# A graph network's last edge pass: edge terms loaded first, table rows gathered onto them by DMA

## The reference

```python
row, col = (edge_index[0], edge_index[1])
h = jnp.concatenate([x[row], edge_attr], axis=1)
h = jax.nn.relu(h @ W1a + b1a) @ W1b + b1b
sums = jax.ops.segment_sum(h, col, num_segments=n_nodes)
counts = jax.ops.segment_sum(jnp.ones((h.shape[0],), dtype=h.dtype), col, num_segments=n_nodes)
agg = sums / jnp.clip(counts, 1.0)[:, None]
z = jnp.concatenate([x, agg, u[batch]], axis=1)
return jax.nn.relu(z @ W2a + b2a) @ W2b + b2b
```

## Time and profile before

| | |
|---|---|
| median of 3 runs | 9359.47 us (9359.37 to 9371.02) |
| profiled execution, first to last instruction (its span) | 9364.4 us |
| first block of the edge pass, within that span | 7146.9 to 8963.4 us |
| PE busy | 7028.5 us (75%) |
| DVE busy | 5660.6 us (60%) |
| POOL busy | 2656.2 us (28%) |
| ACT busy | 2515.7 us (27%) |

### The profile page before, as it was taken

The page is one execution under the profiler, slowest core; times in us unless marked ns, Lnnn a source line. Parts: engine busy times, 40 slices in busy tenths (PEclk is TensorE's granted clock), DMA queues, the critical chain, the costliest instruction groups (busy, mean ns, idle before and its releaser), DMA issues. The chain is left out here.

```text
span 9364.4 us, 133857 instructions
## 1 busy us (share of the span) xinstructions
PE 7028.5 (75%) x35740; PEld 4596.9 (49%) x35792; DVE 5660.6 (60%) x16783; ACT 2515.7 (27%) x5863; POOL 2656.2 (28%) x2952
## 2 busy tenths in 40 slices
PE   4777777775566659940488699999998777777787
PEld 4555555453122224420477544444445666666676
DVE  6777777775589990059899800000014777777786
ACT  0222222222467740020388600000001333310001
POOL 0777777776470000000000000000002444444410
PEclk9767776766679989975799899999999999999998
DMA  3333333334975538849566478787886766642363
GB/s 99 103 103 105 105 104 103 105 105 167 393 231 164 168 114 306 299 195 426 205 215 216 144 262 276 262 287 256 295 284 200 181 180 179 179 111 63 63 178 88
DMA packets 969628, 1759.77 MB, mean 188 GB/s; under 512 B 102288, under 2 KB 665125, under 8 KB 905315
## 3 DMA queue, kind: packets, MB, share of 16 engines
q1 hardware_dynamic: 683820, 1335.73, 44.1%
q0 software_dynamic: 110720, 276.01, 9.0%
q10 hardware_dynamic: 174394, 139.51, 5.5%
HBM read 1412.04 MB, written 338.80 MB: 187 GB/s over the span
## 5 line engine op out<-in xcount | busy, mean ns | idle before, releaser
L768 POOL DMA_INDIRECT bucketed<-arena,wide x1563 | 1515.6, 970 | 726.5 <-issue 714.0
L1920 PE MATMUL psum<-wide,arena 128*128 x6496 | 1209.9, 329 | 400.5 <-DVE arena L1979 393.9
L1920 PEld LDWEIGHTS psum<-wide,arena 128*128 128x128 f32 x6496 | 989.9, 195 | 618.3 <-issue 493.3
L1787 POOL DMA_DIRECT2D table<-wide x13 | 9.7, 743 | 4316.2 <-DVE wide L1711 4316.2
L1979 DVE TENSOR_SCALAR arena<-wide,tile_first 128x128 f32 x3248 | 870.8, 300 | 472.3 <-PE psum L1920 293.8
L1841 POOL DMA_INDIRECT arena<-table,src_i x832 | 803.3, 966 | 1009.1 <-PE psum L1937 872.4
L1660 PE MATMUL psum<-arena,h 128*128 128x512 f32 (+1 forms) x2548 | 1048.6, 570 | 19.1 <-DMA arena<-adjacency 17.5
L922 PE MATMUL psum<-arena 128*128 128x512 bf16 x2253 | 695.7, 442 | 435.0 <-DVE arena L870 259.4
L665 PE MATMUL psum<-arena 128*113 128x177 bf16 x1568 | 534.4, 341 | 416.2 <-ACT wide L687 374.6
L870 DVE TENSOR_SCALAR arena<-sums 128x512 bf16<-128x512 int16 x2304 | 799.9, 347 | 0.0
L659 PE MATMUL psum<-w_edge,arena 128*128 128x256 f32 x1568 | 786.9, 597 | 0.0
(11 more groups left out here) (398 smaller groups left out, 11006.0 us busy)
## 6 DMA issues: line engine op xcount, KB each, us to landing
arena<-adjacency SPq DMA_DIRECT2D x294, 1024.0 KB
arena<-adjacency SPq DMA_DIRECT2D x98, 1568.0 KB, 7.8
adjacency<-wide SPq DMA_DIRECT2D x588, 256.0 KB
arena<-adjacency SPq DMA_DIRECT2D x196, 640.0 KB, 3.9
arena<-adjacency SPq DMA_DIRECT2D x147, 768.0 KB
arena<-bucketed POOLq DMA_DIRECT2D x208, 528.0 KB, 6.0
arena<-adjacency SPq DMA_DIRECT2D x49, 1792.0 KB, 6.9
arena<-adjacency SPq DMA_DIRECT2D x49, 1344.0 KB, 6.1
```

The lines of the kernel that those rows point to most:

```text
L768: e.indirect_dma_start(bucketed, bass.IndirectOffsetOnAxis(ap=places[k][0:size, c:c + 1], axis=0), rows[k][0:size, c, :], None).then_inc(s ...
L1920: e.matmul(flat[:, ds((chunk & 3) * 512 + 2048, P)], lhsT=hot[:, i % 8, :], rhs=table_in[:, ds(tile * P, P)], start=False, stop=True, skip ...
```

## The change

The second ring `edge_in` is gone. SyncE loads the edge terms straight into `ring`, once TensorE is done with what the slot held. GpSimd waits for that landing and gathers with `compute_op=ALU.add`, so that the DMA adds the table rows to what is in the slot. VectorE's addition `message(n)`, its semaphore `s_sum` and the two waits ahead of it are gone; `rectify(n)` waits for the gathers itself, behind `looks(n)`.

```diff
             ring = slots(PAIR * P, DEEP).rearrange("p k (c w) -> p k c w", c=PAIR)
-            edge_in = slots(PAIR * P, DEEP).rearrange("p k (c w) -> p k c w", c=PAIR)
...
                 @block.gpsimd
                     for n in range(FAR_PAIRS):
                         k = n % DEEP
-                        if n >= DEEP:
-                            e.wait_ge(s_pe, n - DEEP + 1)
+                        e.wait_ge(s_side[k], 16 * (n // DEEP + 1))
                         for c in range(PAIR):
                             chunk = (NEAR_PAIRS + n) * PAIR + c
-                            e.indirect_dma_start(ring[:, k, c, :], None, table,
-                                                 bass.IndirectOffsetOnAxis(ap=src_i[:, chunk:chunk + 1], axis=0)).then_inc(s_got[k], 16)
+                            e.indirect_dma_start(ring[:, k, c, :], None, table, bass.IndirectOffsetOnAxis(ap=src_i[:, chunk:chunk + 1], axis=0),
+                                                 compute_op=ALU.add).then_inc(s_got[k], 16)
...
                 @block.sync
                         if n >= DEEP:
-                            e.wait_ge(s_sum, n - DEEP + 1)
-                        e.dma_start(edge_in[:, k, :, :], bucketed_v[:, cols(NEAR_PAIRS + n), 0:D]).then_inc(s_side[k], 16)
+                            e.wait_ge(s_pe, n - DEEP + 1)
+                        e.dma_start(ring[:, k, :, :], bucketed_v[:, cols(NEAR_PAIRS + n), 0:D]).then_inc(s_side[k], 16)
...
                 @block.vector
-                    def message(n):
+                    def rectify(n):
                         k = n % DEEP
                         e.wait_ge(s_got[k], 16 * PAIR * (n // DEEP + 1))
-                        e.wait_ge(s_side[k], 16 * (n // DEEP + 1))
-                        e.tensor_tensor(ring[:, k, :, :], ring[:, k, :, :], edge_in[:, k, :, :], ALU.add).then_inc(s_sum, 1)
-
-                    def rectify(n):
-                        k = n % DEEP
-                        e.wait_ge(s_sum, n + 1)
                         e.tensor_scalar(ring[:, k, :, :], ring[:, k, :, :], 0.0, None, op0=ALU.max).then_inc(s_msg, 1)
...
-                        message(n)
                         if n * PER_PAIR < LOOKS:
                             looks(n)
                         rectify(n)
```

More of the change, by code:

```diff
@@ L1813, in edge_pass @@
             s_side = [sem(f"meta_side{k}") for k in range(DEEP)]
-            s_hot, s_sum, s_msg, s_pe, s_add = (sem("meta_" + n) for n in ("hot", "sum", "msg", "pe", "add"))
+            s_hot, s_msg, s_pe, s_add = (sem("meta_" + n) for n in ("hot", "msg", "pe", "add"))
             sage_groups, sage_loads = 3 * GROUPS, 3 * len(PASSES) * TILES
```

## The result

| | before | after |
|---|---|---|
| median | 9365.92 us (9359.37 to 9377.30, 16 runs) | 9386.92 us (9369.29 to 9398.45, 16 runs) |
| profiled execution, its span | 9364.4 us | 9376.4 us |
| last scatter of the first stage starts (line 768) | 2256.2 us | 2269.0 us |
| first block of the edge pass | 7146.9 to 8963.4 us | 7158.2 to 8975.05 us |
| length of that block | 1816.5 us | 1816.9 us |

The ratio is 1.0019, with a 95% interval of 1.0012 to 1.0027: slower by 11 to 25 us. The block that the change edits (from SyncE's first load in it to its first load in the next one) is as long as it was.

A forecast was written before the change was run, and what follows sets the result against it. TensorE's queue was taken to bound the block. Start -4.0, steady state 0 and end +2.3 gave -1.7 us, from 9359.5 to 9357.8, and 9357 us with a small part of the busy stretch's waits; range 9338 to 9385.

The forecast's parts named there:

- The bound of the block: First block of the edge pass: TensorE's queue of look-ups and register loads is the chain, 4.25 us a quiet pair.
- The addition is worth 0 for each pair: VectorE in each pair: removing its 416 ns addition gains 0 us, as register loads before the first look hide it.
- Order of load and gather, 0: Each pair's gathers now wait for edge terms: 13.7 us at most, inside the ring's 34 us, so cost 0.
- 36 us for "VectorE, or longer register loads": Busy stretch, 240 pairs: 0.15 us a pair of extra TensorE waiting; none taken as gain; rival chance 0.09.
- Issue and transfer of the gathers, 0: GpSimd and DMA engines: adding gathers issue in under 1.5 us, DMA share at most 0.81, all hidden, cost 0.
- Steady state: 0: All pairs between the block's start and end: 0 us of change, between -36 and 0.
- The start, -4.0: Block's start: looks no longer wait behind message(0) for the first gathers, so they begin 4.0 us earlier.
- the 7.15 us: First gather's duration at the block's start, put down to standing behind VectorE's memset; otherwise the gain is about 2 us.
- The end, +2.3, up to +5.1: Last three pairs' gathers wait one edge-load landing, 2.8 to 5.6 us, less 0.5 for the addition gone.
- The sum: Whole kernel: -4.0 + 0 + 2.3 = -1.7 us, with nothing counted outside the edge pass's first block.
- GpSimd as the bound at 9382: Rival, gather issue in each turn: at 1.89 us a gather, quiet pairs pay 24 us, 9382 us; chance 0.14.
- its threshold of 1.8: GpSimd in the quiet stretch: the issue time, 1.8 us a gather, from which GpSimd would decide the pair.

The follow-up runs named there:

- e7: Kernel before, with each look-up's PSUM bank read from a list made beforehand, not computed by TensorE; 9317.71 us, ratio 0.9937.
- e2: Kernel before, with VectorE's addition message(n) moved behind looks(n) for every pair; 9497.34 us, ratio 1.0134.
- e5: Kernel before, with VectorE's addition taken out and both rings kept, so edge terms are left out; 9370.94 us, ratio 0.9995.
- e8: Kernel after, with the same list of PSUM banks as e7; 9297.60 us, ratio 0.9913 against before.
- e11: e7 with SyncE's edge load waiting for TensorE (as in e9) and message(0) behind looks(0), no adding DMA; 9299.86 us, ratio 0.9928 against before.
- e1: Kernel after, with plain gathers without compute_op that overwrite the edge terms; 9353.32 us, ratio 0.9983 against before.
- e9: Kernel before, with only SyncE's edge load made to wait until TensorE is done with the slot; 9360.25 us, ratio 0.9992.
- e3: Kernel before, with compute_op=ALU.add on every gather, onto the slot's old content, VectorE's addition kept; 9405.94 us, ratio 1.0039.
- e4: Kernel before, with compute_op=ALU.add on the two gathers of the last pair alone; 9382.53 us, ratio 1.0014.
- e12: e8 with plain gathers without compute_op, so edge terms are left out; 9260.01 us, ratio 0.9880 against before.
- e10: Kernel before, with VectorE's addition and SyncE's edge loads replaced by one adding direct DMA a pair from GpSimd, gathers plain; 9441.07 us, ratio 1.0079.

## Why the prediction was right and wrong

- **The bound of the block: right.** TensorE's queue was the chain (e7). But the margin, for which I had given no size, was thin: VectorE's turn was 0.12 us shorter (e2), or 0.15 (e7: 4.238 - 4.091).
- **The addition is worth 0 for each pair: right** (e5), and so is its cover, the register loads. The idle time before the first look grew to 0.90 us in the median and not to 1.05, so the looks do start somewhat earlier, and TensorE doesn't care. Without that cover the addition costs 0.33 us a pair (e2), and where VectorE is the chain, being rid of it is worth 0.08 us a quiet pair (e8 against e11).
- **Order of load and gather, 0: right as a price, wrong as a gain.** The ring hid the longer order. The edge loads' new time brought most of 13 us (e1, 8 of them by e9 alone). The prediction's 36 us for "VectorE, or longer register loads" are where they come from: it took none of them, as it looked at VectorE and ScalarE only and had no reason by which register loads would get shorter.
- **Issue and transfer of the gathers, 0: wrong.** I took under 1.5 us and a full cover. Measured are 1.546 us and 13 us of cost in the block (e1 to after, 1803.5 to 1816.9); e3 has 25 us. It was not by GpSimd's or the DMA engines' time, of which both had some left, but in TensorE's queue, whose register loads got longer by what the pairs did. "Steady state: 0" is thus the sum of two terms of 13 us, which is luck. The Trainium skill ("Collectives: The Full Stack", "The bandwidth ceiling: the fold count and why AG ≠ RS ≠ AR") puts two source reads on the add of a collective. The estimate from it, twice the 12.1% of before, is 24%, and the trace agrees in the share, 25.0%. It doesn't show that the reads are the reason: the data packets are eight times as many and an eighth as large, which could double the share as well, and no run separates the two.
- **The start, -4.0: right for the first look (-4.8) and the first sum (-4.5), too high for what stays**, 2.9 us by pair 5. The first gather took 3.92 us and not 7.15, so the 7.15 us weren't its own length. In all fourteen profiles its end is tied to the memset's end: it comes 1.2 us after it if the gather is plain and 1.8 us if it adds, whether the gather starts 0.7 us before the memset or 3.9 us after the memset's start. That it stands behind the memset fits this, but no run moves the memset apart from the rest of the block's begin.
- **The end, +2.3, up to +5.1: right kind, low size.** It is +4.4. The one landing was right: the last six gathers begin 3.0 us later after the sum of pair 405. But each of the six is longer by 0.60 us, which I forgot: from the first to the last start they now take 9.4 us (8958.99 to 8968.41), and took 6.2. Of these 3.2 us, a last landing 1.2 us shorter (4.35 us, before 5.59) gives some back, and the addition gone 0.5.
- **The sum: wrong, as it ended at the block's borders.** It gave -1.7 us for the block, and the block gave +0.4. "The change touches the first block of the edge pass alone, so I read that stretch and leave the shares of the whole page aside": this is the step that failed. In the profiled executions, 12.8 us came from the scatters of the first stage (and 21.4 in e4 against before, 19.6 in e8 against e12), and no rival named them. The rival nearest in time, GpSimd as the bound at 9382, was not what happened: GpSimd kept idle time and waits in each turn, and 1.546 us is below its threshold of 1.8.

Shown is that a DMA that adds, indirect or direct, goes with scatters 9 ns longer in their median in this program (e3, e4, e8, e10 and after, against nine without), and by e4 and e1 that it is the cause. What in GpSimd or in the program does it isn't shown, nor whether it depends on how many such scatters there are.

## What to carry to other kernels

Ask of each new form of instruction what it does to the others of its engine in the whole program, not only beside it: try it once, in a place where it does nothing else (e4), and read the unchanged stages. A net zero over a stretch is not yet "hidden": undo one part at a time, since two terms can cancel. And before taking work off an engine, make sure it is the chain: here the same edit was worth nothing for each pair with TensorE's queue as the chain, and some 20 us behind an edit that shortened that queue (e7 to e8).

## What the runs showed of the hardware

- Two adding gathers in the whole program make 1563 plain scatters longer, from 958 to 968 ns in the median, and leave the plain gathers at 945 ns (e4). Why is open.
- GpSimd is busy 0.945 us with a gather of 128 rows of 512 bytes (before), 1.546 us if it adds (after), and its data then go out in packets of 512 bytes instead of 4096. A direct DMA of 128 KB from GpSimd that adds takes 1.40 us (e10).
- DMAs, between the chip's memory (HBM) and the on-chip SBUF, are issued by SyncE, ScalarE and GpSimd alone in all fourteen traces.
- Register loads in TensorE's queue aren't of fixed length: 590 ns in the mean of the quiet pairs before, 650 (e1) to 719 (e10) in that of the busy ones, and 841 where they overlap ScalarE's issue of a broadcast load (before). They get longer with DMAs that add (e3, after against e1) and shorter with SyncE's load at another time (e9).
- The computation of one address, eight times a turn, held up TensorE by 0.15 us a pair or more (e7).
